# A grouped convolution by blocks of eight unshifted positions, with the outer taps' part moved by one partition

## The chip, the cores and the metric

The kernel runs on one core of one Trainium2 chip. The metric is the device time of one execution in microseconds (us), on the slowest core, here the only one. TensorE (PE), VectorE (DVE), ScalarE (ACT), GpSimd (POOL) and SyncE (SP) run side by side and wait for each other by semaphores.

## What is computed

The input is 8192 rows (128 batches of 64 channels) of 1024 numbers. Two layers follow each other, each of the form x = x + ffn(cond(x)). Cut to what matters:

```python
# layer 0: mix channels with weights that depend on the batch, then the ffn
agg_w = einsum('bk,koi->boi', softmax(mlp(cond)), weight)
y = einsum('boi,bih->boh', agg_w, x) + agg_b[:, :, None]
x = x + (y @ W_base.T + b_base + moe(y))        # 8 experts of rank 16

# layer 1: grouped convolution along the 1024 positions
y = conv(x, weight, padding=4, groups=4)        # 9 taps, 16 channels in a group
y = y + (cond @ c_weight.T)[:, :, None] + fside[None, :, None]
x = x + (y @ base_w.T + base_b + 2 * lora_top2(y))
```

## The kernel before

A step handles one tile of 128 rows (two batches); 64 tiles in layer 0 and then the same 64 in layer 1, so 128 steps. `run` (L177) gives every engine the same list of steps: the first two and last two of each layer are written out, the others are a loop with two steps in its body. Inside a step each engine's instructions stand in a fixed order written by hand in its `step` function, and semaphores do the rest.

Products are made in two parts of a reduced-width type (`hi` and `lo = x - hi`), so that each product is three: hi x hi, hi x lo, lo x hi. In the step of tile n TensorE does (`step`, L856):

- `base` (L796) of tile n for k = 0 to 7: nine matmuls each (three products by three PSUM pieces of 384, 384 and 392 columns), L807.
- `mix` (L762) of tile n+1 after k = 0, 1, 2, 3: one chunk each, a quarter of the tile, into one of two PSUM banks `psT`.
- `turn` of tile n-1 after k = 4 (a transpose) and `up` of tile n-1 after k = 5 (six matmuls of 512 columns, L833), which needs HThi and HTlo of that tile.

In layer 1 `mix` is the convolution. `load_x` (SP, L222) brings x so that partition (r, i) holds position r of a block of eight and channel i of a group, and the free index is channel group and block. It is shifted by four positions: 129 half-shifted blocks for 128, with zeros written at the ends (`pad_zero`). Output position t of a block then needs two neighbouring columns of blocks, w = 0 and 1. For each of them one matmul takes `Xhi` against the hi and lo weights together (256 columns, L787) and one takes `Xlo` against the hi weights (128 columns, L789). The output partition is the block. PSUM then holds two parts, and VectorE's `evacuate_y` (L546) adds first one with the row constant (L566), then the other (L568), into `Y`. One chunk is 256 numbers in each partition.

`Y` is split again: ScalarE rounds each half of 512 to `Yhi` (L431), VectorE makes `Ylo` (L575); in layer 1 both halves wait for all four chunks. The next step's `base` waits for both. ScalarE also rounds the next x to `Xhi` (`high_x`, L417), after which GpSimd makes `Xlo` (L333), and rounds the turned product to `HThi` (L515), after which VectorE makes `HTlo` (L712); then come `add_rest` (L590) and, when `up` is done, `emit` (L605, three adds into `outb`). SP stores `outb`, loads the residual and the next x.

Of the kernel before, what the change touches and what calls it, by code (L numbers as in the profile page):

```python
# [27 lines left out]
P = 128  # L28
# [8 lines left out]
TAPS, PAD = 9, 4  # L37
# [12 lines left out]
QP = Q + 1  # L50
XW = BG * QP
# [17 lines left out]
def build(nc, x, condw, condr, mixw, l0w, l0b, l0B, convw, l1w, l1b, l1B, out):  # L69
# [6 lines left out]
    with ExitStack() as ctx:  # L76
# [11 lines left out]
        CT = sb("CT", [P, G, 2, 2, P], F32R)  # L88
        bias = sb("bias", [P, H])

        Xraw = sb("Xraw", [P, 2, XW])
        Xhi, Xlo = sb("Xhi", [P, XW], F32R), sb("Xlo", [P, XW], F32R)
# [6 lines left out]
        mixT = sb("mixT", [P, MODES, C])  # L99
        prod = sb("prod", [P, MODES, C])  # L100
# [62 lines left out]
        pad_zero = sem("pad_zero")  # L163
# [10 lines left out]
        def as_f32(ap):  # L174
            return ap.bitcast(F32)

# [31 lines left out]
        def _(sp):  # L208
            def load_x(j, par, layer):
# [4 lines left out]
                else:  # L214
# [95 lines left out]
        def _(pool):  # L310
# [8 lines left out]
            pool.memset(stage[:, :, NW - 1:NW], 0.0).then_inc(consts, 1)  # L319

# [46 lines left out]
            def step(j, par, lay0, lay, lay1, lay2):  # L367
# [23 lines left out]
                if isinstance(j, int) and n == 1:  # L391
# [3 lines left out]
                    pool.tensor_tensor(CT[:, :, :, 1, :], craw, as_f32(CT[:, :, :, 0, :]), ALU.subtract)\  # L395
# [6 lines left out]
        def _(act):  # L402
# [4 lines left out]
            def high_x(j, par, layer):  # L407
                n = 2 * j + par
                if layer == 0:
                    act.wait_ge(x_loaded[par], 16 * (j + 1))  # L410
                    w = H
                else:
                    act.wait_ge(g_loaded[par], 16 * BR * (j - STEPS // 2 + 1))
                    w = XW
# [505 lines left out]
```

## Time and profile before

| | us |
|---|---|
| median of 3 runs | 2239.08 |
| lowest and highest | 2237.74, 2240.82 |
| the profiled execution's own time | 2237.36 |
| its span | 2235.6 |
| PE busy | 2193.0, 98% |
| DVE busy | 1394.9, 62% |
| POOL busy | 858.6, 38% |
| ACT busy | 401.7, 18% |
| PE line L807 (base) in the chain that ended last | 73% of the span |
| PE lines L787 and L789 (the convolution) in that chain | 7% and 3% |
| granted TensorE clock, mean | 0.997 |

The span is that of one profiled execution, and the time beside it is the same execution's, 1.8 us longer. The chain that ended last goes back from the last instruction to what released it each time, so an engine's share there is what it contributed to the length; its busy share alone does not say that. In a timeline each line is one instruction or several of a kind; a PEld line is a weight load, which overlaps the matmuls; an engine's name with a q (SPq, ACTq) is its sequencer issuing a DMA.

### The profile page before, as it was taken

The page shows a single profiled execution, that of the slowest core. Times are in us where ns is not written, and L with a number is a line of the kernel's source. Part 1 is how long each engine was busy: PE and PEld are TensorE (multiplying, and loading weights), DVE is VectorE, ACT ScalarE, POOL GpSimd, SP SyncE. Part 2 cuts the span into 40 slices and gives each one's busy share as a digit, 9 for nine tenths or more (in the row PEclk, how much of TensorE's full clock was granted, in tenths as well). Part 3 has the DMA queues.
Part 4 walks back from the last instruction along what each step waited for, and adds up shares of the span by engine and source line. Part 5 has one row for each costly group of instructions (what it writes and reads, how often), then busy time and mean ns, then how long its engine had stood idle before and what let it go on. Part 6 is the DMA issues. An engine that isn't in the chain of part 4 may idle for free.

```text
span 2235.6 us, 40989 instructions
## 1 busy us (share of the span) xinstructions
PE 2193.0 (98%) x13196; PEld 2142.6 (96%) x13196; DVE 1394.9 (62%) x3667; ACT 401.7 (18%) x923; POOL 858.6 (38%) x1053
## 2 busy tenths in 40 slices
PE   4999999999999999999999999999999999999998
PEld 4999999999999999999999999999999999999998
DVE  6777777777777777776655555555555555555554
ACT  3221212121222222222211111111111111111110
POOL 5544444434343434344433333333333333333332
PEclk9999999999999999999999999999999999999999
DMA  5312121111112111213433333334433333333432
GB/s 168 117 60 79 61 73 66 70 70 69 70 69 70 69 70 64 75 60 111 105 93 89 88 88 88 88 88 99 98 94 90 88 88 88 88 88 96 97 95 62
DMA packets 134114, 189.48 MB, mean 85 GB/s; under 512 B 16080, under 2 KB 98384, under 8 KB 134096
## 3 DMA queue, kind: packets, MB, share of 16 engines
q1 hardware_dynamic: 133792, 188.69, 30.3%
q10 hardware_dynamic: 304, 0.56, 0.1%
q8 instruction: 10, 0.16, 0.0%
q14 instruction: 8, 0.07, 0.0%
HBM read 122.01 MB, written 67.18 MB: 85 GB/s over the span
## 4 chain that ended last, share of the span: by engine, by line
PE 96%; DVE 2%; DMA 1%; ACT 1%; issue 0%; POOL 0%; DVEq 0%; SPq 0%; ACTq 0%
PE psB L807 73%; PE psB L833 8%; PE psT L787 7%; PE psT L781 3%; PE psT L789 3%; PE psT L782 1%; PE psB L820 1%; POOL Wlo L324 0%; DVE small L666 0%; DMA outb<-in_condw 0%; DVE prod L526 0%; DMA attb<-att_scratch 0%; ACT Whi L443 0%; DMA Xraw<-in_x 0%; DVE Ylo L575 0%
## 5 line engine op out<-in xcount | busy, mean ns | idle before, releaser
L807 PE MATMUL psB<-Whi,Yhi 128*128 128x384 f32 (+2 forms) x3072 | 748.6, 352 | 3.6 <-issue 3.6
L333 POOL TENSOR_TENSOR Xlo<-Xraw,Xhi 128x256 fp32r<-128x256 f32 (+1 forms) x512 | 423.6, 859 | 785.0 <-ACT Xhi L417 785.0
L807 PE MATMUL psB<-Whi,Ylo 128*128 128x384 f32 (+2 forms) x3072 | 712.3, 340 | 0.0
L807 PE MATMUL psB<-Wlo,Yhi 128*128 128x384 f32 (+2 forms) x3072 | 708.6, 339 | 0.0
L807 PEld LDWEIGHTS psB<-Whi,Ylo 128*128 128x128 f32 x3072 | 558.3, 189 | 0.0
L807 PEld LDWEIGHTS psB<-Wlo,Yhi 128*128 128x128 f32 x3072 | 557.0, 189 | 0.0
L807 PEld LDWEIGHTS psB<-Whi,Yhi 128*128 128x128 f32 x3072 | 517.5, 190 | 19.5 <-issue 3.7
L566 DVE TENSOR_TENSOR Y<-psT,row 128x256 f32<-128x256 f32 x512 | 216.6, 423 | 338.3 <-PE psT L789 318.4
L362 POOL TENSOR_TENSOR res<-res,bias 128x256 f32<-128x256 f32 x256 | 181.5, 742 | 435.5 <-DMA res<-x_scratch 435.5
L431 ACT CAST Yhi<-Y 128x512 fp32r<-128x512 f32 x256 | 159.3, 622 | 897.3 <-DVE Y L568 897.3
L605 DVE TENSOR_TENSOR outb<-psB,res 128x384 f32<-128x384 f32 (+1 forms) x384 | 227.6, 678 | 72.2 <-PE psB L833 65.4
L352 POOL TENSOR_TENSOR res<-Xraw,bias 128x256 f32<-128x256 f32 x256 | 222.8, 903 | 113.9 <-DVE outb L605 113.9
L787 PE MATMUL psT<-CT,Xhi 128*128 128x256 f32 x1024 | 249.0, 320 | 2.6 <-DVE Y L568 1.5
L575 DVE TENSOR_TENSOR Ylo<-Y,Yhi 128x512 fp32r<-128x512 f32 x256 | 212.6, 831 | 46.6 <-ACT Yhi L431 46.6
L789 PE MATMUL psT<-CT,Xlo 128*128 128x128 f32 x1024 | 229.0, 224 | 0.0
L568 DVE TENSOR_TENSOR Y<-psT,Y 128x256 f32<-128x256 f32 x512 | 217.4, 425 | 17.6
L787 PEld LDWEIGHTS psT<-CT,Xhi 128*128 128x128 f32 x1024 | 193.6, 189 | 3.2 <-DVE Y L568 1.8
L789 PEld LDWEIGHTS psT<-CT,Xlo 128*128 128x128 f32 x1024 | 195.3, 191 | 0.0
L417 ACT CAST Xhi<-Xraw 128x1024 fp32r<-128x1024 f32 (+1 forms) x128 | 134.4, 1050 | 163.9 <-PE psT L782 153.8
L781 PE MATMUL psT<-M,Xhi 128*128 128x256 f32 x512 | 132.8, 311 | 21.5 <-DVE M L538 14.9
L699 DVE COPY ag<-psB 128x138 f32<-128x138 f32 (+1 forms) x128 | 38.6, 301 | 167.5 <-PE psB L807 167.5
L781 PEld LDWEIGHTS psT<-M,Xhi 128*128 128x128 f32 x512 | 98.3, 192 | 23.3 <-issue 16.2
(85 smaller groups left out, 1397.7 us busy)
## 6 DMA issues: line engine op xcount, KB each, us to landing
Xraw<-in_x SPq DMA_DIRECT2D x64, 512.0 KB, 3.3
x_scratch<-outb SPq DMA_DIRECT2D x64, 512.0 KB, 2.6
Xraw<-x_scratch SPq DMA_DIRECT2D x512, 64.0 KB, 3.5
res<-x_scratch SPq DMA_DIRECT2D x64, 512.0 KB, 4.7
out<-outb SPq DMA_DIRECT2D x64, 512.0 KB, 3.0
row<-row_scratch SPq DMA_DIRECT2D x128, 64.0 KB, 3.1
stage<-in_l0w SPq DMA_DIRECT2D x8, 580.5 KB, 8.5
stage<-in_l1w SPq DMA_DIRECT2D x8, 580.0 KB, 6.2
```

What stands on the lines that cost most here:

```text
L333: last = pool.tensor_tensor(Xlo[:, piece], Xraw[:, par, piece], as_f32(Xhi[:, piece]), ALU.subtract)
L352: last = pool.tensor_tensor(res[:, par, :].rearrange("p (r q) -> p r q", r=BR)[:, r, :], Xraw[:, par, 0:H].rearrange("p (q r) -> p r q", r ...
L362: last = pool.tensor_tensor(res[:, par, piece], res[:, par, piece], bias[:, piece], ALU.add)
L566: nc.vector.tensor_tensor(y, parts[0], add, ALU.add).then_inc(y_part, 1)
L568: nc.vector.tensor_tensor(y, parts[1], y, ALU.add).then_inc(y_chunk, 1)
L575: nc.vector.tensor_tensor(Ylo[:, par, h * HB:(h + 1) * HB], Y[:, h * HB:(h + 1) * HB], as_f32(Yhi[:, par, h * HB:(h + 1) * HB]), ALU.subtr ...
L605: last = nc.vector.tensor_tensor(to[:, r0:r1, :], product, res[:, par, :].rearrange("p (r q) -> p r q", r=BR)[:, r0:r1, :], ALU.add)
L781: mm(to, Xhi[:, xs], M[:, :, :].rearrange("p s n -> p (s n)"), start=True, stop=False)
L787: mm(to, Xhi[:, xs], CT[:, g, w, :, :].rearrange("p s n -> p (s n)"), start=(w == 0), stop=False)
L789: last = mm(to[:, 0:P], Xlo[:, xs], CT[:, g, w, 0, :], start=False, stop=(w == 1))
L807: last = mm(psB[:, 3 * par + b, 0:cols], y, w[:, k, BANK0[b]:BANK0[b] + cols], start=(k == 0 and y is yh and w is Whi), stop=(k == KT - 1 ...
L833: last = mm(psB[:, 3 * par + b, :], y[:, :], w[:, layer, b * HB:(b + 1) * HB], start=False, stop=(y is HTlo), skip_group_check=True)
```

## The change

The blocks are no longer shifted: block q holds positions 8q to 8q+7. The tap matrices now have a part w = 0, by which a block gives to its own outputs, and a part w = 1, by which it gives to its neighbours' (outputs 0 to 3 of block q+1, outputs 4 to 7 of block q-1). Both parts stand side by side in one 256-column operand, so a block takes three matmuls of 256 columns, and PSUM adds hi and lo products itself. Since the output partition is the block, the w = 1 part has to move by one partition:

- VectorE adds the w = 0 part of each chunk and the row constant into `Y`, one add in place of two.
- ScalarE copies the w = 1 part of each chunk to `side` (`copy_side`).
- After every second chunk ScalarE issues four DMAs (`shift`), SBUF to SBUF, into `shifted`: outputs 0 to 3 one partition up, outputs 4 to 7 one down, each as a piece of 112 and one of 15 partitions, 1 KB in each.
- VectorE adds each half of `shifted` to `Y` (`add_shifted`) once its DMAs have landed.
- The halves of `Y` are now those of the channel groups' blocks, so half 0 can be split after two chunks. On ScalarE `high_ht` now comes ahead of `high_x`; on VectorE `Ylo` of half 1 comes after `emit`.
- `mixT` and `prod`, used in layer 0 only, share their memory with `side`. The zero columns and `pad_zero` are gone, and x is loaded with 1024 instead of 1032 numbers.

Layer 0's order is as it was.

```diff
+HALF_B = BG // 2
+SHIFT_ROWS = ((0, 112), (112, P - 1))
+SHIFTS = 2 * 16 * len(SHIFT_ROWS)
...
@@ load_x
-                        first = 1 if r < PAD else 0
-                        sp.dma_start(dst[r * GC:(r + 1) * GC, :, first:first + Q], src[(r + PAD) % BR])\
-                            .then_inc(g_loaded[par], 16)
+                        sp.dma_start(dst[r * GC:(r + 1) * GC, :, :], src[r]).then_inc(g_loaded[par], 16)
...
@@ scalar
+            def copy_side(j, par, c):
+                m = 2 * j + par - STEPS
+                act.wait_ge(y_chunk, NC * (m + STEPS) + c + 1)
+                if isinstance(m, int) and m == 0:
+                    act.wait_ge(agg_ready, STEPS)
+                else:
+                    act.wait_ge(side_in, SHIFTS * (2 * m + c // 2 - 1))
+                bank = psT[:, c % 2, :].rearrange("p (b s t o) -> p b s t o", b=2, s=2, t=BR)
+                to = side[:, c // 2, :, :].rearrange("p t (b o) -> p b t o", b=HALF_B)
+                b = 2 * (c % 2)
+                nc.scalar.copy(to[:, b:b + 2], bank[:, :, 1]).then_inc(side_out, 1)
+
+            def shift(j, par, h):
+                m = 2 * j + par - STEPS
+                act.wait_ge(side_out, NC * m + 2 * h + 2)
+                if isinstance(m, int) and m == 0:
+                    act.wait_ge(side_zero, 1)
+                else:
+                    act.wait_ge(y_sum, 2 * m + h - 1)
+                for p0, p1 in SHIFT_ROWS:
+                    act.dma_start(shifted[p0 + 1:p1 + 1, h, 0:REACH, :], side[p0:p1, h, 0:REACH, :])\
+                        .then_inc(side_in, 16)
+                    act.dma_start(shifted[p0:p1, h, REACH:BR, :], side[p0 + 1:p1 + 1, h, REACH:BR, :])\
+                        .then_inc(side_in, 16)
...
@@ scalar, step
-                if last_of_0:
-                    for k in range(KT // 2):
-                        split_w(k, 1)
+                for c in range(NC):
+                    if last_of_0:
+                        split_w(c, 1)
+                    if lay1 == 1:
+                        copy_side(*after(j, par), c)
+                        if c % 2:
+                            shift(*after(j, par), c // 2)
                 if lay1 is not None:
                     split_y(*after(j, par), lay1, range(0, 1))
+                if lay1 == 1 and lay0 is not None:
+                    high_ht(*before(j, par))
                 if lay2 is not None and not last_of_0:
                     high_x(j + 1, par, lay2)
-                if lay0 is not None:
+                if lay1 != 1 and lay0 is not None:
                     high_ht(*before(j, par))
...
@@ vector, evacuate_y in layer 1: one add
+                        nc.vector.tensor_tensor(y, bank[:, :, 0], add, ALU.add).then_inc(y_chunk, 1)
+            def add_shifted(j, par, h):
+                m = 2 * j + par - STEPS
+                dve.wait_ge(side_in, SHIFTS * (2 * m + h + 1))
+                dve.wait_ge(y_chunk, NC * (m + STEPS) + 2 * h + 2)
+                y = y_half(Y[:, :], 1, h)
+                nc.vector.tensor_tensor(y, shifted[:, h, :, :], y, ALU.add).then_inc(y_sum, 1)
...
@@ tensor, mix
+                if layer == 1 and not (isinstance(j, int) and n == STEPS and c < 2):
+                    pe.wait_ge(side_out, NC * (n - STEPS) + c - 1)
...
-                        g = k % G
-                        for w in range(2):
-                            xs = slice(k * QP + w, k * QP + w + Q)
-                            mm(to, Xhi[:, xs], CT[:, g, w, :, :].rearrange("p s n -> p (s n)"),
-                               start=(w == 0), stop=False)
-                            last = mm(to[:, 0:P], Xlo[:, xs], CT[:, g, w, 0, :], start=False, stop=(w == 1))
+                        hi, lo = (CT[:, k % G, s, :, :].rearrange("p w n -> p (w n)") for s in range(2))
+                        mm(to, Xhi[:, xs], hi, start=True, stop=False)
+                        mm(to, Xhi[:, xs], lo, start=False, stop=False)
+                        last = mm(to, Xlo[:, xs], hi, start=False, stop=True)
```

How the order of instructions changes in a step of layer 1. ScalarE before, one whole step of the loop (L427, L430, L416: register work and waits):

```order
L510 ACTIVATE small<-small 128x1 [waits diff_ready]
L427 REGISTER_ALU
L430 REGISTER_ALU [waits base_done]
L431 CAST Yhi<-Y 128x512 [waits y_chunk]
L416 ISA [waits g_loaded1]
L417 CAST Xhi<-Xraw 128x1032 [waits mixed]
L515 CAST HThi<-psB 128x128 [waits tr_done]
L431 CAST Yhi<-Y 128x512 [waits y_chunk]
```

and with the change, the end of the same step's copies and what follows them (L448 the copy, L459 and L461 the DMAs of `shift` for half 1, L435 Yhi, L551 HThi; Xhi follows):

```order
L440 REGISTER_ALU
L448 COPY mixbuf<-psT 128x2x8x16 [waits side_in,y_chunk]
L453 REGISTER_ALU
L459 DMA shifted<-mixbuf 112x256 [waits y_sum,side_out]
L461 DMA shifted<-mixbuf 112x256
L459 DMA shifted<-mixbuf 15x256
L461 DMA shifted<-mixbuf 15x256
L429 REGISTER_ALU
L434 REGISTER_ALU [waits base_done]
L435 CAST Yhi<-Y 128x8x64 [waits y_sum]
L551 CAST HThi<-psB 128x128 [waits tr_done]
```

What stood first after the fourth chunk, Yhi, now stands behind a copy and four issues, and HThi behind Yhi as before but ahead of Xhi.

VectorE before, from the fourth chunk's second add (L568) to `emit` (L605), with L575 Ylo and L712 HTlo:

```order
L568 TENSOR_TENSOR Y<-psT,Y 128x2x8x16
L574 REGISTER_ALU
L575 TENSOR_TENSOR Ylo<-Y,Yhi 128x512
L712 TENSOR_TENSOR HTlo<-psB,HThi 128x128
L590 TENSOR_TENSOR res<-psB,res 128x256
L574 REGISTER_ALU
L575 TENSOR_TENSOR Ylo<-Y,Yhi 128x512
L598 REGISTER_ALU
L605 TENSOR_TENSOR outb<-psB,res 128x3x128 x2
L605 TENSOR_TENSOR outb<-psB,res 128x2x128
```

and with the change, the third and fourth chunk's adds (L603) and between them the add of `shifted` for half 0 (L611):

```order
L603 TENSOR_TENSOR Y<-psT,row 128x2x8x16
L608 ISA
L611 TENSOR_TENSOR Y<-shifted,Y 128x8x64
L589 REGISTER_ALU
L603 TENSOR_TENSOR Y<-psT,row 128x2x8x16
```

and right behind these (L617 Ylo, L753 HTlo, L646 `emit`):

```order
L616 REGISTER_ALU
L617 TENSOR_TENSOR Ylo<-Y,Yhi 128x8x64
L753 TENSOR_TENSOR HTlo<-psB,HThi 128x128
L631 TENSOR_TENSOR res<-psB,res 128x256
L608 ISA
L611 TENSOR_TENSOR Y<-shifted,Y 128x8x64
L639 REGISTER_ALU
L646 TENSOR_TENSOR outb<-psB,res 128x3x128 x2
L646 TENSOR_TENSOR outb<-psB,res 128x2x128
L616 REGISTER_ALU
L617 TENSOR_TENSOR Ylo<-Y,Yhi 128x8x64
```

The add of the shifted half 0 stands ahead of the fourth chunk's add, and Ylo of half 1 has moved from ahead of `emit` to behind it.

TensorE, one mixing chunk before:

```order
L787 MATMUL psT<-CT,Xhi 128x256
L789 MATMUL psT<-CT,Xlo 128x128
L787 MATMUL psT<-CT,Xhi 128x256
L789 MATMUL psT<-CT,Xlo 128x128
L787 MATMUL psT<-CT,Xhi 128x256
L789 MATMUL psT<-CT,Xlo 128x128
L787 MATMUL psT<-CT,Xhi 128x256
L789 MATMUL psT<-CT,Xlo 128x128
```

and with the change:

```order
L834 MATMUL psT<-CT,Xhi 128x256
L835 MATMUL psT<-CT,Xhi 128x256
L836 MATMUL psT<-CT,Xlo 128x256
L834 MATMUL psT<-CT,Xhi 128x256
L835 MATMUL psT<-CT,Xhi 128x256
L836 MATMUL psT<-CT,Xlo 128x256
```

Eight matmuls of two widths have become six of one.

## Rows read from the trace of the kernel before

**Rows 1.** The page, parts 1 and 4: busy time and share; chain that ended last.

```profile
PE 2193.0 (98%) x13196; PEld 2142.6 (96%) x13196; DVE 1394.9 (62%) x3667; ACT 401.7 (18%) x923; POOL 858.6 (38%) x1053
...
PE 96%; DVE 2%; DMA 1%; ACT 1%; issue 0%; POOL 0%; DVEq 0%; SPq 0%; ACTq 0%
```

**Rows 2.** Timeline of PE, 1702 to 1726: start, us, engine, line, out<-in, shape, count.

```profile
1702.02 0.69 PE L833 MATMUL psB<-Bhi,HThi 128*128 128x512 f32 x2
...
1703.49 0.69 PE L807 MATMUL psB<-Whi,Yhi 128*128 128x384 f32 x3
...
1706.68 0.69 PE L807 MATMUL psB<-Whi,Yhi 128*128 128x384 f32 x3
...
1708.43 0.33 PE L787 MATMUL psT<-CT,Xhi 128*128 128x256 f32 x1
1708.61 0.23 PE L789 MATMUL psT<-CT,Xlo 128*128 128x128 f32 x1
1708.67 0.34 PE L787 MATMUL psT<-CT,Xhi 128*128 128x256 f32 x1
...
1716.68 0.74 PE L807 MATMUL psB<-Whi,Yhi 128*128 128x384 f32 x3
...
1720.02 0.69 PE L833 MATMUL psB<-Bhi,HThi 128*128 128x512 f32 x2
```

**Rows 3.** Timeline of DVE in the same step; idle time before it in brackets.

```profile
1703.78 2.19 DVE L605 TENSOR_TENSOR outb<-psB,res 128x384 f32<-128x384 f32 x3 [0.99 <-PE psB L833]
...
1716.88 0.42 DVE L566 TENSOR_TENSOR Y<-psT,row 128x256 f32<-128x256 f32 x1 [1.64 <-PE psT L789]
...
1718.45 0.69 DVE L575 TENSOR_TENSOR Ylo<-Y,Yhi 128x512 fp32r<-128x512 f32 x1 [0.69 <-ACT Yhi L431]
1719.57 0.29 DVE L712 TENSOR_TENSOR HTlo<-psB,HThi 128x128 fp32r<-128x128 f32 x1 [0.43 <-ACT HThi L515]
```

**Rows 4.** Timeline of ACT in the same step.

```profile
1717.80 0.62 ACT L431 CAST Yhi<-Y 128x512 fp32r<-128x512 f32 x1 [10.11 <-DVE Y L568]
1718.32 1.05 ACT L417 CAST Xhi<-Xraw 128x1032 fp32r<-128x1032 f32 x1
1719.28 0.26 ACT L515 CAST HThi<-psB 128x128 fp32r<-128x128 f32 x1
```

**Rows 5.** Stretches: us, PE, PEld, DVE, ACT, POOL busy, PEclk, DMA share, GB/s.

```profile
1710.70:1712.50 1.80, 1.80 (x15) 1.80 (x14) 0.62 (x2) 0.00 (x0) 0.97 (x2) 1.00 1.00 163
1712.50:1714.20 1.70, 1.70 (x15) 1.70 (x13) 0.23 (x1) 0.00 (x0) 1.70 (x3) 1.00 0.42 74
```

**Rows 6.** Timeline of PEld, weight loads inside one mixing chunk.

```profile
1708.61 0.19 PEld L787 LDWEIGHTS psT<-CT,Xhi 128*128 128x128 f32 x1
1708.72 0.19 PEld L789 LDWEIGHTS psT<-CT,Xlo 128*128 128x128 f32 x1
```

**Rows 7.** Lines L222 and L224 on SP, 1300 to 2100: duration ns min/median/max.

```profile
L222 SPq DMA_DIRECT2D Xraw<-x_scratch x352: 316/317/347, 1311.8 to 2089.4; - x176
...
L224 SPq DMA_DIRECT2D row<-row_scratch x44: 351/352/352, 1316.0 to 2089.9; - x44
```

**Rows 8.** Timelines of ACT and SP in the prologue.

```profile
1.18 1.16 ACTq L405 DMA_DIRECT2D mixT<-in_mixw  x2
2.37 1.28 ACT L447 ACT_TABLE_LOAD   x1 [2.37 <-issue]
...
51.21 0.59 SPq L279 DMA_DIRECT2D stage<-in_convw  x1
```

**Rows 9.** DMA issues: count, KB each, median us from issue to landing.

```profile
Xraw<-x_scratch SPq DMA_DIRECT2D x512, 64.0 KB, 3.5
...
att_scratch<-Y SPq DMA_DIRECT2D x1, 4.0 KB, 2.0
```

**Rows 10.** Timeline of POOL, 1716 to 1726.

```profile
1719.45 3.34 POOL L333 TENSOR_TENSOR Xlo<-Xraw,Xhi 128x258 fp32r<-128x258 f32 x4 [5.11 <-ACT Xhi L417]
```

**Rows 11.** Timeline of PE at the border between the layers.

```profile
1083.51 0.39 PE L787 MATMUL psT<-CT,Xhi 128*128 128x256 f32 x1 [1.48 <-DVE Y L568]
```

More of the change, by code:

```diff
@@ L88, in build @@
         CT = sb("CT", [P, G, 2, 2, P], F32R)
+        shifted = sb("shifted", [P, 2, BR, HALF_B * GC])
         bias = sb("bias", [P, H])
-        Xraw = sb("Xraw", [P, 2, XW])
-        Xhi, Xlo = sb("Xhi", [P, XW], F32R), sb("Xlo", [P, XW], F32R)
+        Xraw = sb("Xraw", [P, 2, H])
+        Xhi, Xlo = sb("Xhi", [P, H], F32R), sb("Xlo", [P, H], F32R)
         Y = sb("Y", [P, H])
@@ L98, in build @@
         attb = sb("attb", [P, STEPS, MODES])
-        mixT = sb("mixT", [P, MODES, C])
-        prod = sb("prod", [P, MODES, C])
+        mixbuf = sb("mixbuf", [P, 2, MODES * C])
+        mixT, prod = (mixbuf[:, i, :].rearrange("p (k o) -> p k o", k=MODES) for i in range(2))
+        side = mixbuf[:, :, :].rearrange("p h (t n) -> p h t n", t=BR)
         agg = sb("agg", [P, C])
@@ L175, in as_f32, with y_half @@
             return ap.bitcast(F32)
+        def y_half(ap, layer, h):
+            if layer == 0:
+                return ap[:, h * HB:(h + 1) * HB]
+            return ap.rearrange("p (t n) -> p t n", t=BR)[:, :, h * HALF_B * GC:(h + 1) * HALF_B * GC]
         def run(eng, step):
@@ L410, in high_x @@
                     act.wait_ge(x_loaded[par], 16 * (j + 1))
-                    w = H
                 else:
                     act.wait_ge(g_loaded[par], 16 * BR * (j - STEPS // 2 + 1))
-                    w = XW
                 if not (isinstance(n, int) and n == 0):
                     act.wait_ge(mixed, NC * n)
-                nc.scalar.copy(Xhi[:, 0:w], Xraw[:, par, 0:w]).then_inc(x_hi, 1)
+                nc.scalar.copy(Xhi[:, :], Xraw[:, par, :]).then_inc(x_hi, 1)
             def high_m(n):
@@ L734, in step @@
                     split_y(*after(j, par), lay1, range(0, 1))
+                if lay1 == 1:
+                    add_shifted(*after(j, par), 0)
                 if lay1 is not None:
@@ L741, in step @@
                     add_rest(*before(j, par))
-                if lay1 is not None:
+                if lay1 == 0:
                     split_y(*after(j, par), lay1, range(1, 2))
+                if lay1 == 1:
+                    add_shifted(*after(j, par), 1)
                 if lay2 == 0:
@@ L749, in step @@
                     emit(*before(j, par), lay0)
+                if lay1 == 1:
+                    split_y(*after(j, par), lay1, range(1, 2))
             run(dve, step)
@@ L794, in base @@
                 n = 2 * j + par
-                if k % (KT // 2) == 0:
+                if layer == 0 and k % (KT // 2) == 0:
                     pe.wait_ge(yhi_half, 2 * n + 1 + 2 * k // KT)
                     pe.wait_ge(ylo_half, 2 * n + 1 + 2 * k // KT)
+                if layer == 1 and k == 0:
+                    pe.wait_ge(yhi_half, 2 * n + 2)
+                    pe.wait_ge(ylo_half, 2 * n + 2)
                 if k == 0 and not (isinstance(j, int) and j == 0):
```

65 lines of the change are left out of this document (30 added, 35 removed).

## The prediction

> All clocks below are microseconds; T counts from the first base matmul of a second-layer step, which stands at 1706.68 in the step that I read.
>
> **What bounds the kernel now.** I began with the page: TensorE is busy 98% of the span and makes up 96% of the chain that ended last [rows 1]. So every step has TensorE's length, and the other engines only matter where they make it wait. Next I took TensorE's instructions in order of time in the second half: `up` starts at 1702.02 and again at 1720.02, so a second-layer step is 18.00, and over many steps it is 17.99 [rows 2]. `up` takes 1.46 to 1.47 (the next base part starts at 1703.49), and two base parts of nine matmuls reach to 1706.68, 1.59 each. Eight of those, `up` and a transpose of 0.08 leave 17.99 - 12.72 - 1.46 - 0.08 = 3.73 for the four mixing chunks, 0.93 each. Read directly, four base parts and four chunks take 1716.68 - 1706.68 = 10.00, which makes 0.91, so the closure holds to 0.02.
>
> Then I looked at who is nearly late. `up` starts at 1720.02 [rows 2], and the low half of the turned product ends on VectorE at 1719.86 [rows 3], only 0.16 earlier. Behind that is ScalarE, which between chunk 3 and `up` does Yhi at 1717.80, Xhi at 1718.32 and HThi at 1719.28, and nothing for 10.11 before [rows 4]. ScalarE is 18% busy, but its work sits exactly in the stretch where `up` waits for it. That stretch decides this change.
>
> **What TensorE saves.** Per block, two pairs of one 256-wide and one 128-wide matmul become three 256-wide ones: the columns are the same, 768, the matmuls fall from four to three, and per step from 32 to 24. A pair takes 0.234 (a 256-wide one starts at 1708.43, the next at 1708.67) [rows 2], far over its 384 columns at the full clock of 2.4 GHz (granted 1.00 [rows 5]), 0.160. The weight loads start every 0.11 to 0.12 there [rows 6], and that is what paces a pair. For a 256-wide matmul in a row with others there is no row. Lower end: the load's pace, 0.117. Upper end: the 0.18 from the 256-wide start at 1708.43 to the 128-wide one behind it at 1708.61 [rows 2]. Nearest are 384-wide ones: nine with 386.7 columns on average take 1.59, 0.177 each, of which 0.161 is columns and 0.016 is fixed. 256 columns make 0.107 + 0.016 = **0.124**, above the load's pace, and I take that. A chunk becomes 6 x 0.124 = 0.744, a step saves 4 x (0.93 - 0.744) = 0.74, and TensorE alone would need 17.24. Over the 64 mixed tiles that is 47. The page "TensorE: Matmul & The Clock Gate" of the Trainium skill (Back-to-back issue gap) gives 262 cycles, 0.109, for 256 columns. No row here shows that pace; the 0.016 that the 384-wide ones show over their columns speaks against it.
>
> **What VectorE saves and gets.** Four second adds of 0.42 like the first ones go [rows 3]; two adds over 512 elements come. Ylo, the same engine, size and operand types, takes 0.69 [rows 3]; I take 0.65 in a row of instructions, since neighbours overlap a little. It has room: what counts is only where the adds stand, as below.
>
> **What ScalarE gets.** Four copies of 256 elements out of PSUM: between HThi's 128 elements at 0.26 and Yhi's 512 at 0.62 [rows 4] lies 0.39. And eight DMA issues in a step. An issue is not free: in the steady loop SyncE spends 317 ns on each piece of Xraw and 352 on `row` [rows 7], and in the prologue 0.59 on each small one of the conv weights [rows 8]. ScalarE's own two at the start take 1.16 together, 0.58 each, and its table load starts at 2.37, 0.03 behind them, so an issue holds up what follows [rows 8]. Ends: 0.35 and 0.64 with a gap of 0.03 to 0.05. The pieces are one plain run in each partition, like `row` with its 0.352, so I take 0.35 + 0.04 = **0.39 each**, 1.56 a half. From issue to landing the ends are 2.0 (4 KB, quiet) and 3.5 (Xraw, behind full DMA engines) [rows 9]. The DMA engines are full to T = 5.8 and at 0.42 to T = 7.5 [rows 5]; the pieces come at T = 5.8 to 7.4 and after 10.8, so mostly quiet, and I take **2.2**, near the lower end.
>
> **The chain, walked by T.** Chunk 1 ends at 2 x 1.59 + 2 x 0.744 = 4.67. VectorE starts 0.20 after a chunk (1716.68 to 1716.88) [rows 2, 3], adds to 5.29; copy to 5.72; issues start at 5.80, the fourth at 6.97, and lands at about 9.2. VectorE, in its order, adds the shifted half first, to 9.90, and only then takes chunk 3, which had ended at 9.34: 0.36 lost. Then: add 10.32, copy 10.75, four issues from 10.80 to 12.4, Yhi of half 0 to 13.0, HThi behind it, Ylo of half 0 on VectorE 13.04 to 13.69, HTlo 13.94, `up` at 14.0. TensorE is ready for `up` at T = 12.60 (8 parts before it). **It stands 1.4**, twice what the narrower mixing saved. Moving Xhi (1.05) behind HThi, which the change also does, is in this already. Behind `up`: it ends at 15.46, the output adds run from 15.75 to 17.94 (three took 2.19 [rows 3]), and now Ylo of half 1 stands behind them, to 18.62, so that the next base matmul starts at 18.70 instead of TensorE's own 15.46 + 3.18 = 18.64. Xhi is done at 14.2, GpSimd's Xlo (four pieces, 3.34 [rows 10]) at 17.6, and it is wanted at 20.3: covered. The second landing, 14.2, is covered by `add_rest` and `up`; without that cover it would go into Ylo of half 1.
>
> So a step is **18.70 against 17.99, +0.71**, and there are 63 of them: +44.7. At the border of the layers the engines around TensorE already are late (it stood 1.48 for a chunk to be emptied [rows 11]) and ScalarE gets eight issues and four copies more, 4.7 of work, some of it beside waiting: +3, between 0 and 8. Sum +48. Everything in the first layer stays. On the profiled execution's 2237.4 that is 2285; the median of the runs shown is 1.7 higher, so I say **2287**.
>
> **How it scales.** As long as the first half's landing is late, seven issues lie on the chain (three before the fourth of half 0, four of half 1), so 0.10 on each issue moves the step by 0.7; break-even is an issue of 0.29. Each 0.1 on the landing moves it 0.1. An issue of 0.50 gives 19.47, +93 over the 63; a landing of 3.0 gives 19.50, +95. An issue of 0.35 with a landing of 2.0 and the load's pace of 0.117 gives 18.13, +9 and the border's 3.
>
> **Rivals.**
> (A) *The issues do not hold ScalarE.* If each costs it 0.20 or less, only 4 of them lie on the chain, the landing of half 0 is in time, and the step is 17.58: -26, to 2213; at 0.10 TensorE and the output adds set 17.3, -43, 2196. It decides below 0.29. Against it: every issue row is 0.317 or more [rows 7, 8], ScalarE's own among them. For it: ScalarE issues nothing in the steady loop, so none of these rows is of that case. Chance 0.22. The page "DMA: Bandwidth & Descriptors" of the Trainium skill (Issuing engines are not separate DMA queues) says that the sequencer's time for starting a DMA is usually small beside the DMA itself, which would be this case.
> (B) *The landing is what is late*: rows of 1 KB between partitions behind half-full DMA engines take 3.0 or more; VectorE then stands before `shifted` with chunk 3 queued behind it. 19.50 a step, +95, 2337; with 3.5 2370 and more. Chance 0.13.
> (C) *It cancels*: issues of 0.28 to 0.30, step 17.93 to 18.00, within 4 of before. Chance 0.07.
> (D) *Three 256-wide matmuls are no faster*: at 0.174 a chunk is 1.04, which delays the walk above by 0.84, the step 19.54, 2340. Nothing speaks for it but the gap between two starts. Chance 0.03.
> The forecast itself, issues of 0.31 to 0.5 with a landing near 2.2: 0.55.
>
> **How the numbers follow.** Faster is A, 0.22; within 0.2% (about 4.5, what a measurement of this kernel can tell) is C, 0.07; slower is the rest, 0.71. The range starts inside A at an issue of 0.20, 2213, and ends above B and the 0.50 issue, 2345; outside are A's cheaper half and the far ends of B and of the issue price.
>
> **What would show it.** Right: a second-layer step of 18.4 to 19.0; ScalarE issues of 0.33 to 0.40 each, four in a row before Yhi; TensorE idle 1 to 1.8 before `up`, released by HTlo; CT matmuls starting every 0.12; VectorE's first shifted add waiting for a DMA. Wrong: a step of TensorE's length without idle time at `up` (A), or the wait sitting at the shifted add for over 1 (B). The forecast falls if an issue lasts under 0.29 on ScalarE.

## The result, and the profile after

| | before | after |
|---|---|---|
| median of 4 runs, us | 2238.46 | 2537.99 |
| lowest and highest | 2237.74, 2240.82 | 2534.32, 2538.78 |
| span of the profiled execution | 2235.6 | 2532.2 |
| granted TensorE clock, mean | 0.997 | 0.946 |

The ratio is 1.1333, 95% interval 1.1313 to 1.1352. The forecast was slower, 2287 within 2213 to 2345; the kernel is slower, but by 300 instead of 48.

The page of the changed kernel, its first line and the clock's, which answer to [rows 1]:

```profile
PE 2266.4 (90%) x12684; PEld 2188.9 (86%) x12684; DVE 1347.4 (53%) x3539; ACT 502.2 (20%) x1179; POOL 858.5 (34%) x1052
...
PEclk9999999999999999989989899989999989899988
```

TensorE's share has fallen from 98% to 90%, while its busy time has grown by 73 although it has 512 matmuls fewer. In the second half the clock's digit is 8 in eight of the slices; before it is 9 in all 40. Both losses are seen in one step. The timeline of PE in a step of layer 1, to be laid beside [rows 2] (L834 to L836 the convolution, L857 `base`, L883 `up`):

```profile
1702.58 0.28 PE L834 MATMUL psT<-CT,Xhi 128*128 128x256 f32 x1
1702.69 0.28 PE L835 MATMUL psT<-CT,Xhi 128*128 128x256 f32 x1
1702.81 0.28 PE L836 MATMUL psT<-CT,Xlo 128*128 128x256 f32 x1
...
1707.92 0.69 PE L857 MATMUL psB<-Whi,Yhi 128*128 128x384 f32 x3
...
1710.69 0.71 PE L857 MATMUL psB<-Whi,Ylo 128*128 128x384 f32 x3
1714.82 0.70 PE L883 MATMUL psB<-Bhi,HThi 128*128 128x512 f32 x2 [3.41 <-DVE HTlo L753]
...
1716.35 1.17 PE L857 MATMUL psB<-Whi,Yhi 128*128 128x384 f32 x3
1717.32 1.17 PE L857 MATMUL psB<-Wlo,Yhi 128*128 128x384 f32 x3
1718.29 1.17 PE L857 MATMUL psB<-Whi,Ylo 128*128 128x384 f32 x3
1719.25 0.86 PE L857 MATMUL psB<-Whi,Yhi 128*128 128x384 f32 x3
1719.95 0.69 PE L857 MATMUL psB<-Wlo,Yhi 128*128 128x384 f32 x3
```

The convolution's matmuls start every 0.11 to 0.12, so a block's three matmuls of 256 columns take 0.36, where its two pairs of [rows 2] took 0.47. The fourth chunk ends at 1707.92, where the fifth base part starts. After the sixth base part TensorE stands 3.41, until HTlo. Behind `up`, three matmuls take 0.97 where they took 0.53 before and again from 1719.95 on. The stretches of the same step (columns as in [rows 5]):

```profile
1711.40:1714.80 3.40, 0.00 (x1) 0.02 (x1) 1.02 (x3) 1.68 (x3) 0.00 (x0) 1.00 0.22 65
...
1716.30:1719.30 3.00, 3.00 (x11) 2.94 (x10) 2.58 (x4) 0.00 (x0) 1.97 (x3) 0.50 0.00 0
```

TensorE does nothing in the first and runs at 0.50, that is 1.2 GHz, in the second, right behind. The wait is there in every step; the view of the waits from 1400 to 2400 (engine and line, releaser, total us, times, longest):

```profile
PE psB L883 <- DVE HTlo L753: 153.2, 45, 3.5
```

153.2 in 45 steps is 3.40 a step. Who is late is on ScalarE. Its timeline between the fourth chunk and `up`, beside [rows 4]:

```profile
1709.57 0.37 ACT L448 COPY mixbuf<-psT 128x256 f32<-128x256 f32 x1 [1.69 <-DVE Y L603]
1709.97 0.57 ACTq L459 DMA_DIRECT2D shifted<-mixbuf  x1
1710.57 0.62 ACTq L461 DMA_DIRECT2D shifted<-mixbuf  x1
1711.22 0.84 ACTq L459 DMA_DIRECT2D shifted<-mixbuf  x1
1712.09 0.84 ACTq L461 DMA_DIRECT2D shifted<-mixbuf  x1
1713.12 0.62 ACT L435 CAST Yhi<-Y 128x512 fp32r<-128x512 f32 x1 [3.18 <-issue]
1713.65 0.26 ACT L551 CAST HThi<-psB 128x128 fp32r<-128x128 f32 x1
```

After the copy come the four issues, 0.57, 0.62, 0.84 and 0.84 (0.72 in the mean), 2.99 with their gaps, and only then Yhi and HThi. VectorE in the same step, beside [rows 3]:

```profile
1708.51 0.69 DVE L611 TENSOR_TENSOR Y<-shifted,Y 128x512 f32<-128x512 f32 x1 [2.30 <-DMA shifted<-mixbuf]
1709.12 0.42 DVE L603 TENSOR_TENSOR Y<-psT,row 128x256 f32<-128x256 f32 x1
1713.78 0.69 DVE L617 TENSOR_TENSOR Ylo<-Y,Yhi 128x512 fp32r<-128x512 f32 x1 [4.24 <-ACT Yhi L435]
1714.38 0.28 DVE L753 TENSOR_TENSOR HTlo<-psB,HThi 128x128 fp32r<-128x128 f32 x1
```

The add of the shifted half 0 waits for its DMA, and the fourth chunk's add behind it starts at 1709.12, 1.2 after the chunk's end, where VectorE otherwise starts 0.20 after one. So 1.0 is lost there before ScalarE's copy can begin, and Ylo of half 0 waits 4.24 for ScalarE. The landing itself is short; the page's DMA part and the view of the DMAs, beside [rows 9]:

```profile
shifted<-mixbuf ACTq DMA_DIRECT2D x256, 112.0 KB, 2.3
...
shifted<-mixbuf ACTq DMA_DIRECT2D x256, 15.0 KB, 2.0
```

From here on "a step" is the mean distance between the starts of `up` over 59 steps of layer 1: 17.99 before, **22.46** after.

### The profile page after: what moved, and what is told of

It reads as the page before. It is cut to its first block and busy times, and to the rows that moved or that the text cites. A ratio compares the mean times of both kernels' runs of the same rounds, so it can differ in the third digit from the quotient of the medians.

```text
span 2532.2 us, 41392 instructions
## 1 busy us (share of the span) xinstructions
PE 2266.4 (90%) x12684; PEld 2188.9 (86%) x12684; DVE 1347.4 (53%) x3539; ACT 502.2 (20%) x1179; POOL 858.5 (34%) x1052
## 5 line engine op out<-in xcount | busy, mean ns | idle before, releaser
L344 POOL TENSOR_TENSOR Xlo<-Xraw,Xhi 128x256 fp32r<-128x256 f32 x512 | 423.6, 858 | 1062.6 <-ACT Xhi L419 1062.6
L857 PE MATMUL psB<-Whi,Yhi 128*128 128x384 f32 (+2 forms) x3072 | 763.2, 358 | 4.4 <-issue 4.4
L857 PE MATMUL psB<-Wlo,Yhi 128*128 128x384 f32 (+2 forms) x3072 | 732.7, 348 | 0.0
L857 PE MATMUL psB<-Whi,Ylo 128*128 128x384 f32 (+2 forms) x3072 | 730.2, 347 | 0.0
L857 PEld LDWEIGHTS psB<-Wlo,Yhi 128*128 128x128 f32 x3072 | 577.1, 195 | 0.0
L857 PEld LDWEIGHTS psB<-Whi,Ylo 128*128 128x128 f32 x3072 | 576.2, 194 | 0.0
L857 PEld LDWEIGHTS psB<-Whi,Yhi 128*128 128x128 f32 x3072 | 548.8, 200 | 28.5 <-issue 5.6
L617 DVE TENSOR_TENSOR Ylo<-Y,Yhi 128x512 fp32r<-128x512 f32 x256 | 212.3, 830 | 272.3 <-ACT Yhi L435 272.3
L883 PE MATMUL psB<-Bhi,HThi 128*128 128x512 f32 x256 | 103.0, 489 | 224.4 <-DVE HTlo L753 224.4
L646 DVE TENSOR_TENSOR outb<-psB,res 128x384 f32<-128x384 f32 (+1 forms) x384 | 222.0, 662 | 127.2 <-PE psB L883 119.2
L883 PEld LDWEIGHTS psB<-Bhi,HThi 128*128 128x128 f32 x256 | 50.1, 224 | 244.0 <-ACT HThi L551 244.0
L435 ACT CAST Yhi<-Y 128x512 fp32r<-128x512 f32 x256 | 159.0, 621 | 512.5 <-DVE Y L598 259.3
L603 DVE TENSOR_TENSOR Y<-psT,row 128x256 f32<-128x256 f32 x256 | 108.1, 423 | 238.3 <-PE psT L836 235.3
L448 ACT COPY mixbuf<-psT 128x256 f32<-128x256 f32 x256 | 95.4, 373 | 562.8 <-DVE Y L603 361.4
L611 DVE TENSOR_TENSOR Y<-shifted,Y 128x512 f32<-128x512 f32 x128 | 88.7, 693 | 149.2 <-DMA shifted<-mixbuf 149.2
L419 ACT CAST Xhi<-Xraw 128x1024 fp32r<-128x1024 f32 x128 | 134.2, 1048 | 166.4 <-PE psT L831 157.6
L834 PE MATMUL psT<-CT,Xhi 128*128 128x256 f32 x512 | 144.2, 282 | 2.0 <-ACT mixbuf L448 1.1
L836 PE MATMUL psT<-CT,Xlo 128*128 128x256 f32 x512 | 144.5, 282 | 0.0
L835 PE MATMUL psT<-CT,Xhi 128*128 128x256 f32 x512 | 144.1, 281 | 0.0
```

What stands on the lines that cost most here:

```text
L344: last = pool.tensor_tensor(Xlo[:, piece], Xraw[:, par, piece], as_f32(Xhi[:, piece]), ALU.subtract)
L419: nc.scalar.copy(Xhi[:, :], Xraw[:, par, :]).then_inc(x_hi, 1)
L435: nc.scalar.copy(y_half(Yhi[:, par, :], layer, h), y_half(Y[:, :], layer, h)).then_inc(yhi_half, 1)
L617: nc.vector.tensor_tensor(y_half(Ylo[:, par, :], layer, h), y_half(Y[:, :], layer, h), as_f32(y_half(Yhi[:, par, :], layer, h)), ALU.subtr ...
L646: last = nc.vector.tensor_tensor(to[:, r0:r1, :], product, res[:, par, :].rearrange("p (r q) -> p r q", r=BR)[:, r0:r1, :], ALU.add)
L834: mm(to, Xhi[:, xs], hi, start=True, stop=False)
```

## The experiments

### The change without its DMAs

```diff
 def copy_side:
-                    act.wait_ge(side_in, SHIFTS * (2 * m + c // 2 - 1))
+                    act.wait_ge(y_sum, 2 * m + c // 2 - 1)
 def add_shifted:
-    dve.wait_ge(side_in, SHIFTS * (2 * m + h + 1))
+    dve.wait_ge(side_out, NC * m + 2 * h + 2)
-    nc.vector.tensor_tensor(y, shifted[:, h, :, :], y, ALU.add).then_inc(y_sum, 1)
+    nc.vector.tensor_tensor(y, side[:, h, :, :], y, ALU.add).then_inc(y_sum, 1)
 scalar step:
-                        if c % 2:
-                            shift(*after(j, par), c // 2)
```

> Leaves out the move by one partition: no DMAs, VectorE adds the copied part in place, at the wrong partition. Everything else of the change stays, the narrower mixing, the copies, the order. Theory (the DMA issues on ScalarE are the whole loss, the rest of the change is good): no idle TensorE at `up`, a step of 4 chunks of 0.714, 8 base parts of 1.59, `up` 1.46 and the transpose, 17.2, against 17.99: about -50, 2189. Rival (the copies and the new order on VectorE cost by themselves): idle time before `up` or before the first base matmul stays, a step of 17.5 or more, 2208 or more.

Measured: 2195.31, ratio 0.9808 (0.9792 to 0.9824), a step of 17.24 in the mean (about 17.17 and 17.32 by turns). For `up` (L877 here) the waits from 1400 to 2200 hold one line, a single wait of 0.8:

```profile
PE psB L877 <- DVE HTlo L747: 0.8, 1, 0.8
```

The theory holds, with a time 6 above its 2189. So matmuls, copies, the two adds and the new order are 43 faster than before, and everything that was lost, 343 against this kernel, is lost by eight DMAs a step: their issues, their landings and what the clock does behind the wait.

### Only the pieces of 112 rows

```diff
-SHIFT_ROWS = ((0, 112), (112, P - 1))
+SHIFT_ROWS = ((0, 112),)
```

> Leaves out the pieces of 15 rows, so the last rows' outer part is not added. Two issues per half instead of four. Theory (ScalarE's issue time, 0.59 and 0.63 for the 112-row pieces): 1.25 instead of 2.95 before Yhi, TensorE idle 0.5 to 0.9 before `up`, no drop of the granted clock, step 17.7 to 18.1, 2222 to 2246. Rival (the time is the landing of the DMAs, not their issue): the first shifted add still waits 2 or more and the idle time at `up` stays above 2, step 19.5 or more, 2330 or more.

Measured: 2262.16, ratio 1.0107 (1.0090 to 1.0124), a step of 18.21, no drop of the clock. The waits from 1400 to 2200:

```profile
DVE Y L611 <- DMA shifted<-mixbuf: 59.8, 44, 2.3
...
PE psB L883 <- DVE HTlo L753: 31.4, 44, 1.6
```

Idle before `up` is 31.4 / 44 = 0.71, inside what the theory gave; time and step came out 16 and 0.1 above it. The other theory is out: the shifted adds wait 59.8 / 44 = 1.4 where they waited 2.3, and no longer 2 or more. The pieces of 15 rows, an eighth of the data but half of the issues and the dearer half, cost 276 of the 343, the loss by the clock among it.

### The issues of half 1 behind HThi

```diff
 scalar step:
-                        if c % 2:
-                            shift(*after(j, par), c // 2)
+                        if c == 1:
+                            shift(*after(j, par), 0)
                 ...
                 if lay1 == 1 and lay0 is not None:
                     high_ht(*before(j, par))
+                if lay1 == 1:
+                    shift(*after(j, par), 1)
```

> On ScalarE the four issues of half 1 come after Yhi of half 0 and HThi instead of ahead of them; nothing else. Theory (position of the issues ahead of HThi): idle time before `up` falls from 3.4 to 0.1 to 0.4, but half 1 lands later, its add stands ahead of the output adds on VectorE, and TensorE waits 2.2 to 2.8 before the next base part: step 19.6 to 20.2 while the granted clock stays full, 2345 to 2380; if that wait also lowers the clock, up to 1.7 more a step, 2480. Rival (order on ScalarE does not matter, DMA landing does): step above 21.5, 2460 or more, with the idle time still at `up`.

Measured: 2316.61, ratio 1.0347 (1.0330 to 1.0365), a step of 19.04, clock full. The waits from 1400 to 2200 (L859 `base`, L885 `up`):

```profile
PE psB L859 <- DVE Ylo L619: 52.3, 42, 1.3
...
PE psB L885 <- DVE HTlo L755: 4.2, 22, 0.5
```

The idle time at `up` is gone, as the theory had it, and a wait of 1.25 stands before the next base part instead. That is half of the 2.2 to 2.8 that I gave, so the step is below the range. What counts here: all eight issues are still made, all on ScalarE, and 221 of the 300 are gone by moving four of them behind two casts, Yhi of half 0 and HThi.

### SyncE issues

```diff
 sync step, behind load_x, ahead of store:
+                if lay1 == 1:
+                    for h in range(2):
+                        shift(*after(j, par), h)      # the same, with sp. for act.
 scalar step:
-                        if c % 2:
-                            shift(*after(j, par), c // 2)
```

> The same eight DMAs of a step issued by SyncE, between its load of the next x and its store; ScalarE only copies. Theory A (an issue of this shape costs what it costs on ScalarE, 0.57 to 0.84, anywhere): half 0 lands around 10.0 after the start of a step, half 1's issue ends around 14, Ylo of half 1 comes behind the output adds, step 19.0 to 19.6, 2305 to 2340. Theory B (the high price is ScalarE's, SyncE issues them in 0.32 to 0.37 like its other ones): both halves land in time, step 17.2 to 17.3, about 2190.

Measured: 2334.74, ratio 1.0430 (1.0413 to 1.0448), a step of 19.33. SyncE's own timeline:

```profile
1713.77 0.58 SPq L319 DMA_DIRECT2D shifted<-mixbuf  x1
1714.49 0.55 SPq L321 DMA_DIRECT2D shifted<-mixbuf  x1
1715.08 0.86 SPq L319 DMA_DIRECT2D shifted<-mixbuf  x1
1715.99 0.82 SPq L321 DMA_DIRECT2D shifted<-mixbuf  x1
```

Theory A, in step and time. TensorE's waits from 1400 to 2300 are 63.8 in 46 steps before the next base part and 14.2 in 46 at `up`. SyncE, which issues its loads in 0.32 to 0.35 and its store in 0.39 in this same loop, needs 0.58, 0.55, 0.86 and 0.82 for these. The price belongs to the transfer and not to ScalarE.

### What an issue costs by its shape

Eight extra issues on SyncE, in its idle time, in the kernel before:

```diff
+                    sp.dma_start(pdst[0:128, 0, :], psrc[0:128, :])
+                    sp.dma_start(pdst[0:112, 1, :], psrc[0:112, :])
+                    sp.dma_start(pdst[1:113, 2, :], psrc[0:112, :])
+                    sp.dma_start(pdst[1:65, 3, :], psrc[0:64, :])
+                    sp.dma_start(pdst[1:17, 4, :], psrc[0:16, :])
+                    sp.dma_start(pdst[1:16, 5, :], psrc[0:15, :])
+                    sp.dma_start(pdst[0:15, 6, :], psrc[0:15, :])
+                    sp.dma_start(pdst[1:9, 7, :], psrc[0:8, :])
```

> The kernel before, with eight extra small DMAs a step that SyncE issues in its idle time in the second layer, all inside on-chip memory, 256 bytes in each partition, results unused: 128 rows in place, 112 in place, 112, 64, 16 and 15 rows moved by one partition, 15 in place, 8 moved. Theory (the price of an issue is that of a transfer from on-chip memory to on-chip memory, and a number of rows that is not a multiple of 16 adds to it): 128, 112, 64 and 16 rows 0.55 to 0.62 each, in place or moved, 15 and 8 rows 0.80 to 0.86. Rival (the price is that of the move by one partition): in place 0.32 to 0.37, moved 0.55 and over. Second rival (the price follows the rows): 16 rows well under 112. The time of the kernel itself should stay within 1% of before, since SyncE is idle for 11.9 in a step of 17.99.

Measured: 2240.67 in one execution, the kernel before beside it 2238.41. SyncE's timeline, in the order of the diff:

```profile
1715.54 0.54 SPq L289 DMA_DIRECT2D pdst<-psrc  x1
1716.12 0.59 SPq L290 DMA_DIRECT2D pdst<-psrc  x1
1716.76 0.60 SPq L291 DMA_DIRECT2D pdst<-psrc  x1
1717.40 0.60 SPq L292 DMA_DIRECT2D pdst<-psrc  x1
1718.04 0.59 SPq L293 DMA_DIRECT2D pdst<-psrc  x1
1718.68 0.87 SPq L294 DMA_DIRECT2D pdst<-psrc  x1
1719.60 0.82 SPq L295 DMA_DIRECT2D pdst<-psrc  x1
1720.46 0.68 SPq L296 DMA_DIRECT2D pdst<-psrc  x1
```

128, 112, 64 and 16 rows cost 0.54 to 0.60 whether moved or in place, 15 rows 0.82 to 0.87, as the theory had it; 8 rows cost 0.68, less than it gave. Neither the bytes nor the partition decide it. Nor is it only that 15 and 8 rows stand last here: the second of two issues takes 0.62 where it moves 112 rows (the kernel with these pieces alone) and 0.82 to 0.88 where it moves 15 (the kernel with two sequencers, below).

The same with one end in device memory:

```diff
+                    sp.dma_start(pd[0, 0:128, :], psrc[0:128, :])     # then 112, 16, 15 rows
+                    sp.dma_start(pdst[0:128, 0, :], x[0:128, 0:64])   # then 112, 16, 15 rows
```

> As e5_shapes, but each extra small DMA has one end in device memory: 128, 112, 16 and 15 rows of 256 bytes from on-chip to device memory, and the same from device to on-chip memory (results unused). Theory (the dear issue, 0.54 to 0.60 for multiples of 16 rows, is that of transfers with both ends on chip): 128, 112 and 16 rows 0.32 to 0.40 each, 15 rows 0.55 to 0.65. Rival (it is the fixed address or the short run, not the two ends): 0.54 to 0.60 again for 128, 112 and 16 rows, 0.82 to 0.88 for 15.

Measured: 2238.97 in one execution, the kernel before beside it 2239.00. Issues of 112, 16 and 15 rows out of the chip's memory, and of 15 rows into it (duration in ns, min/median/max):

```profile
L292 SPq DMA_DIRECT2D probe_scratch<-psrc x50: 429/429/434, 1301.6 to 2182.2; - x50
...
L293 SPq DMA_DIRECT2D probe_scratch<-psrc x50: 427/427/436, 1302.1 to 2182.7; - x50
...
L294 SPq DMA_DIRECT2D probe_scratch<-psrc x50: 432/433/443, 1302.6 to 2183.2; - x50
...
L298 SPq DMA_DIRECT2D pdst<-in_x x50: 432/433/441, 1304.4 to 2185.0; - x50
```

128 rows cost 350 ns out and 374 ns in. So for these plain shapes an issue with one end outside costs 0.35 to 0.43, with both ends inside 0.54 to 0.60: the theory's direction, with 112 and 16 rows a little above its 0.40. The extra for 15 rows, 0.28 with both ends inside, is 0.005 here, which is not what the theory said. One end outside does not make every issue cheap either: the 0.59 and 0.58 of [rows 8] load from device memory too, the conv weights in pieces of 16 partitions with several short runs in each, and why they are dearer was not tested. The page "DMA: Bandwidth & Descriptors" of the Trainium skill (Why a DMA increments its semaphore by 16 and not by 1) says that a DMA of 15 partitions runs on 15 engines and that the sequencer then writes the missing count itself. By this measurement that writing alone cannot be the 0.28, since it would stand in both. What the 0.28 is stays open.

### What an idle TensorE costs

Into the kernel before, unused copies of 512 elements on ScalarE ahead of HThi, three and six:

```diff
+                if lay == 1 and not isinstance(j, int):
+                    for f in range(3):                # 6 in the other
+                        act.wait_ge(filled, 3 * (n - STEPS - 1) + f)
+                        nc.scalar.copy(prod[:, :, :], mixT[:, :, :]).then_inc(filled, 1)
                 if lay0 is not None:
                     high_ht(*before(j, par))
```

> The kernel before, with three copies of 512 elements that nothing uses on ScalarE ahead of HThi, in 60 steps of the second layer: it measures what an idle TensorE costs ahead of `up`. Theory (an idle time of this length costs only itself): idle 1.6 to 1.9 before `up`, granted clock 1.00 as before, step 19.6 to 19.9, 2335 to 2355. Rival (any wait lowers the clock): step above 20.8, 2405 or more.

> The same with six copies, so that TensorE stands about as long as in the changed kernel. Theory (the idle time is long enough to lower the granted clock to a half for a stretch behind it, and that is the missing 1.7 of the changed kernel's step): idle 3.5 to 3.9, records of 0.50 in each step, step 23.2 to 23.7, 2550 to 2580. Rival (the drop of the clock comes from the changed kernel's DMAs or matmuls, not from the idle time): idle the same, granted clock 1.00, step 21.5 to 21.9, 2450 to 2475.

Measured: three copies 2345.83, ratio 1.0478 (1.0457 to 1.0499), a step of 19.77, clock 0.997; six copies 2550.78, ratio 1.1394 (1.1369 to 1.1418), a step of 23.12, clock 0.957. The first matmuls of `up` with three copies:

```profile
1702.74 0.71 PE L839 MATMUL psB<-Bhi,HThi 128*128 128x512 f32 x2 [1.65 <-DVE HTlo L718]
1703.29 0.62 PE L839 MATMUL psB<-Blo,HThi 128*128 128x512 f32 x2
```

and with six:

```profile
1713.14 1.19 PE L839 MATMUL psB<-Bhi,HThi 128*128 128x512 f32 x2 [3.60 <-DVE HTlo L718]
1714.13 1.05 PE L839 MATMUL psB<-Blo,HThi 128*128 128x512 f32 x2
```

Idle 1.65 costs 19.77 - 17.99 = 1.78, little more than itself. Idle 3.60 costs 23.12 - 17.99 = 5.13 in the mean, that is 1.53 more than itself, and the matmuls behind it take 0.99 a pair instead of 0.55. The mean hides several kinds of step. The wait is 3.60 in each, but 12 steps of the 59 have no record of 0.50 and last 21.75, inside what the rival gave; 34 last 23.3, 12 last 24.1 to 24.3, and the last one, with no wait at its end, 20.5. So the theory's "in each step" is missed, and its step by 0.1. A fall of the clock costs 23.3 - 21.75 = 1.55 in most cases and 2.4 to 2.5 in 12; without one the wait costs 0.16 more than itself. What decides whether it falls in a given step stays open. No DMA and no matmul was changed in this kernel, and three copies leave the clock full, so the fall of the clock needs neither the DMAs nor the new matmuls, only the longer wait.

### Two sequencers, and a version that beats both

First the eight issues shared, ScalarE those that go up, SyncE those that go down, and Yhi of half 0 ahead of the fourth copy:

```diff
 ScalarE's shift:
-                    act.dma_start(shifted[p0:p1, h, REACH:BR, :], side[p0 + 1:p1 + 1, h, REACH:BR, :])
 SyncE's shift, same waits:
+                    sp.dma_start(shifted[p0:p1, h, REACH:BR, :], side[p0 + 1:p1 + 1, h, REACH:BR, :])
 scalar step:
+                        if c == 3:
+                            split_y(*after(j, par), lay1, range(0, 1))
```

> The changed kernel with the eight DMAs shared: ScalarE issues the pieces that go one partition up, SyncE those that go down, two each per half; and ScalarE makes Yhi of half 0 ahead of the fourth chunk's copy, so that HThi stands behind two issues only. By the measured issues (0.57 to 0.62 and 0.84) half 0 is issued from 5.3 to 6.8 after the step's start and landed at 8.2, before the fourth chunk ends at 9.3; half 1 from 10.3 to 11.8, landed at 13.2, before `up` ends at 14.0; HThi at 12.0, HTlo by 12.4. Theory: no idle time over 0.2 at `up` and 0.2 or less before the next base part, step 17.2 to 17.5, 2190 to 2212, faster than both kernels. Rival (two sequencers issuing at once slow each other down, or the landings get late): issues over 1.0, idle time of 0.5 or more at `up`, step 17.9 or more, 2235 or more.

Measured: 2250.65, ratio 1.0050 (1.0034 to 1.0067), a step of 18.00. The theory is missed, and the step and time are the rival's, by one half of its reason: the issues kept their price, but a landing is late, and 0.49 a step stayed at `up`. VectorE's timeline tells why (L626 the shifted add, L618 the fourth chunk, L768 HTlo):

```profile
1710.85 0.69 DVE L626 TENSOR_TENSOR Y<-shifted,Y 128x512 f32<-128x512 f32 x1 [1.60 <-DMA shifted<-mixbuf]
1711.46 0.42 DVE L618 TENSOR_TENSOR Y<-psT,row 128x256 f32<-128x256 f32 x1
...
1714.37 0.29 DVE L768 TENSOR_TENSOR HTlo<-psB,HThi 128x128 fp32r<-128x128 f32 x1 [1.44 <-ACT HThi L566]
```

The fourth chunk, whose last matmul was followed by the next base part at 1710.96, still stood behind the landing of half 0. Then the order on VectorE and ScalarE was changed:

```diff
 vector step:
+                    evacuate_y(*after(j, par), lay1, range(3, NC))
                     add_shifted(*after(j, par), 0)
-                    evacuate_y(*after(j, par), lay1, range(3, NC))
-                    split_y(*after(j, par), lay1, range(0, 1))
                     low_ht(*before(j, par))
                     add_rest(*before(j, par))
+                    split_y(*after(j, par), lay1, range(0, 1))
 scalar step: Yhi of half 0 behind HThi
 side_in: one semaphore for each half
```

> e8_two with two moves: VectorE adds the fourth chunk ahead of the shifted half 0, so that the fourth chunk's copy and the issues behind it do not wait for a landing, and Yhi and Ylo of half 0 come behind HThi and HTlo. Each half has a semaphore of its own. Theory (the 0.46 at `up` in e8_two came from the fourth chunk waiting behind the first landing): no idle time at `up`, under 0.2 before the next base part, step 17.2 to 17.4, 2198 to 2212. Rival (two issues of 1.43 on ScalarE keep HThi late anyway): 0.3 or more at `up`, step 17.6 or more, 2225 or more.

Measured: **2215.51, ratio 0.9895 (0.9879 to 0.9912)** to before, a step of 17.50: 1% faster than the kernel before, and faster than the changed one. Its page:

```profile
PE 2163.5 (98%) x12684; PEld 2093.1 (95%) x12684; DVE 1365.9 (62%) x3539; ACT 502.8 (23%) x1179; POOL 839.7 (38%) x1052
```

TensorE is back at 98%. No matmul of `up` waits any more from 1400 to 2200, and for the landings this is left there:

```profile
DVE Y L627 <- DMA shifted<-mixbuf: 0.2, 1, 0.2
```

The step is 0.1 above my range and the time 3.5, and the step is 0.26 above the kernel without DMAs. Laid beside that kernel's, the matmuls' starts show 0.16 of the 0.26 ahead of the next tile's first base matmul, which in the step that I read waits for Ylo of half 1 behind the output adds. Why that comes later here was not followed further.

## Why the prediction was wrong

**What bounds, and where it would break.** Right. TensorE sets the step, the stretch between the fourth chunk and `up` decides, and ScalarE is what is late there; every link of the walk is found in the timelines in that order. (The "8 parts" beside T = 12.60 should be six; the sum is right.)

**TensorE's saving.** Right. A 256-wide matmul takes 0.119, against 0.124 taken; the step without a wait is 17.24 in the mean, as forecast. The 0.109 of the Trainium skill's page "TensorE: Matmul & The Clock Gate" (Back-to-back issue gap) is not reached here.

**VectorE's adds, the copies, the landing.** Right: 0.69 against 0.65 for the add; 0.37 against 0.39; 2.3 and 2.0 against 2.2.

**The price of an issue. This is the term that failed.** "The pieces are one plain run in each partition, like `row` with its 0.352, so I take 0.35 + 0.04". They cost 0.57, 0.62, 0.84 and 0.84. I chose the near row by the shape of the run, and for plain runs what decides is that both ends lie on chip, which no row of the kernel before had; 15 rows then cost 0.28 more than 16, beyond even the upper end of 0.64. That the conv weights' 0.59 and ScalarE's own 0.58 come near the 112-row price is no more than chance as far as is known, since they load from device memory. With the measured issues the same walk has 0.95 more before the fourth issue of half 0 and 1.43 more in half 1's four, so 1.4 + 2.4 = 3.8 at `up`, for 3.40 measured (3.58 between the matmuls' starts, since the view models a matmul's end). The rest is in terms taken a little long: the first issue stands at T = 5.68 for 5.80, and the last of half 0 lands after 2.0 for 2.2.

**The clock, which no step of the prediction had.** I priced an idle TensorE at its own length. 22.46 is 17.24 + 3.40 + 1.82. About 1.55 of the 1.82 is the granted clock at 0.50 behind the wait: from start to start, `up` and the base matmuls of a step take that much longer than in the kernel with the 112-row pieces alone, whose clock stays full. The other 0.27 is not the clock; the same sum leaves 18.21 - 17.24 - 0.71 = 0.26 in that kernel. The filler runs show the same without the change: an idle time of 1.65 leaves the clock alone, one of 3.60 brings a fall in most steps, which costs 1.55 or more. The page "TensorE: Matmul & The Clock Gate" of the Trainium skill warns of this (Why this matters for your kernels: idle gaps between bursts of matmuls bring the half clock back), and the trace agrees: 0.50 behind 3.40. At the forecast's 1.4 it would not have mattered, so I did not ask what happened beyond; "0.10 on each issue moves the step by 0.7" holds only as far as the clock does. With the issues at 0.64, the end that I kept, the formula gave 20.45 and about 2397, outside my range, which I had cut at 0.50.

**The border.** 64 distances between the starts of `up`, from before the border on, are 289 longer; 64 x 4.47 is 286, so 3 are left for the border, as forecast. The rest of the 296.6 between the spans is 4 in layer 0, 1.4 ahead of it and 1.9 at the end. Of the 4, 1.7 lie in the first distance, which differs by up to 2.2 between these kernels, and 2.4 are a step of 16.13 instead of 16.09. All seven kernels that have the change show 16.13, the one without DMAs too; so does the one with six filler copies (16.12), but not those with three or with extra issues. So it does not need the change, and its cause is open.

**The rivals.** A, cheap issues, is refuted by the timelines and by SyncE's issues. B, late landings, is refuted: 2.3 and 2.0, and with the 112-row pieces alone, which land no sooner (2.4), the step is 18.21. The sign I had given for B, over 1 of wait at the shifted add, was badly chosen: it is met, with 2.30, but by my own walk the third chunk's add ends at T = 7.6 and the landing is at 9.2, so the forecast itself has 1.6 there. The wait grew because the fourth issue is late, not the landing. C would need issues of 0.30 and D matmuls of 0.174; the timelines show 0.57 or more and 0.119.

## What to carry to other kernels

Price a DMA issue by its two ends, its number of rows and its shape, and measure one of exactly that kind before building on it; the sequencer's time in front of a dependent instruction counts in full, even on an engine that is 20% busy. When a walk says that TensorE will stand, ask also whether the wait is long enough to cost the clock behind it, because then the loss grows faster than the wait. And a sound idea can lose by where four issues stand: the same eight transfers gave 2538, 2317 and, over two sequencers with the waits put last, 2216.

## What the runs showed of the hardware

- An issue of a plain shape with both ends on chip took 0.54 to 0.60 on SyncE for 16, 64, 112 or 128 rows, and 0.52 to 0.63 on ScalarE for 112; with one end in device memory it took 0.35 to 0.43 on SyncE for 15, 16, 112 or 128 rows. Other loads from device memory, at the start, took 0.58 and 0.59.
- With both ends on chip 15 rows took 0.82 to 0.88 on either sequencer and 8 rows 0.68, more than 16 or 128 rows. With one end in device memory 15 rows took 0.43, as 16 did; 8 were not tried.
- TensorE idle for 1.65 in each step kept a granted clock of 0.997; idle for 3.4 it came back at 0.50 in every step, idle for 3.6 in 47 steps of 59. Beside the wait that cost 1.55 a step in the mean in the first case, and 1.55 in the most frequent step of the second.
- 256-wide matmuls with a weight load each follow at 0.119, the pace at which the loads came before as well.
